# One of the 32 chunks of maxima of a group copied by ACT and folded by Pool

## The reference

```
x = x + attn_a(ln(x))   # 32 heads of 8, biases, plain softmax over 1024 keys
x = x + ffn(ln(x))      # silu gate x up (256 -> 1024), 2:4 sparsified, down
x = x + attn_b(ln(x))   # 32 heads of 8 on 8 key/value heads, -1e10 on keys with i-128 <= j < i
x = x + ffn(ln(x))
```

## Time and profile before

| | us |
|---|---|
| median of 3 runs (1656.22 to 1662.11) | 1660.44 |
| the profiled execution | 1661.54 |
| its span, first to last instruction | 1659.6 |
| PE busy | 1611.3 (97%) |
| DVE busy | 1490.8 (90%) |
| ACT busy | 1282.2 (77%) |
| Pool busy | 267.5 (16%) |

### The profile page before, as it was taken

How to read it: one execution, slowest core, us unless ns; L and a number is a source line. 1 busy time by engine, 2 the same in 40 slices (tenths; PEclk the granted TensorE clock), 3 DMA queues, 4 the chain that set the end, 5 groups by cost and what they waited for, 6 DMA issues and landing times.

```text
span 1659.6 us, 39596 instructions
## 1 busy us (share of the span) xinstructions
PE 1611.3 (97%) x14128; PEld 638.9 (38%) x14128; DVE 1490.8 (90%) x2168; ACT 1282.2 (77%) x2424; POOL 267.5 (16%) x623
## 2 busy tenths in 40 slices
PE   6899999999999999999988999999999999999999
PEld 3322222222222223777753222222222222247777
DVE  6999999999999997787777999999999999938765
ACT  3399999999999998433224999999999999983321
POOL 1410000000000000000012223333322233320000
PEclk9999999999999999999997999999999999999999
DMA  6943344334354321200404322222223222111000
GB/s 161 295 99 70 63 77 83 63 65 84 68 141 87 71 60 44 64 1 1 117 15 132 64 60 57 51 58 60 55 55 67 63 51 52 55 53 55 14 13 26
DMA packets 72126, 114.70 MB, mean 69 GB/s; under 512 B 12464, under 2 KB 27824, under 8 KB 71984
## 3 DMA queue, kind: packets, MB, share of 16 engines
q1 hardware_dynamic: 71984, 112.63, 29.2%
HBM read 71.96 MB, written 40.63 MB: 68 GB/s over the span
## 4 chain that ended last, share of the span: by engine, by line
PE 56%; DVE 32%; issue 7%; DMA 2%; ACT 1%; SPq 1%; DVEq 0%; POOLq 0%; ACTq 0%
DVE mneg L1305 28%; PE psum L785 18%; PE psum L767 11%; PE psum L737 7%; PE psum L887 6%; PE psum L843 6%; PE psum L848 3%; PE psum L700 2%; PE psum L823 2%; DVE area L1355 1%; PE psum L682 1%; PE psum L720 1%; DMA area<-k_stacks 0%; DVE stats L1198 0%; SPq L461 0%
## 5 line engine op out<-in xcount | busy, mean ns | idle before, releaser
L1055 ACT ACTIVATE area<-psum 128x512 f32<-128x512 f32 x2048 | 1097.2, 600 | 42.1 <-PE psum L767 14.6
L785 PE MATMUL psum<-area 128*32 128x256 f32 x8192 | 655.4, 392 | 0.4 <-POOL area L1567 0.4
L767 PE MATMUL psum<-area 51*128 51x512 bf16 x2048 | 638.9, 385 | 2.4 <-DVE vsb_b L1255 1.4
L1311 DVE CUSTOM_DVE_ANT_0 xn<-psum,band 128x1024 f32<-128x1024 f32 x512 | 588.4, 1235 | 12.6 <-PE psum L737 11.3
L1305 DVE TENSOR_REDUCE mneg<-psum 128x1 f32<-128x1024 f32 x512 | 581.0, 1209 | 7.1 <-PE psum L737 7.1
L785 PEld LDWEIGHTS psum<-area 128*32 128x32 f32 x8192 | 162.0, 108 | 400.9 <-issue 259.2
L737 PE MATMUL psum<-area 48*128 48x512 bf16 x1024 | 301.2, 386 | 8.0 <-DVE mneg L1305 4.6
L767 PEld LDWEIGHTS psum<-area 51*128 51x128 bf16 x2048 | 141.1, 94 | 426.5 <-ACT area L1055 353.6
L737 PE MATMUL psum<-k_max_b,area 48*128 48x512 bf16 x1024 | 292.5, 385 | 6.1 <-DVE mneg L1311 5.0
L1548 POOL TENSOR_TENSOR mparts<-mneg,nought 128x16 bf16<-128x16 f32 x64 | 14.2, 222 | 741.6 <-DVE mneg L1305 500.5
L1100 ACT ACTIVATE area<-psum 128x512 f32<-128x512 f32 x64 | 38.2, 600 | 120.0 <-PE psum L848 119.9
(11 more groups left out here) (89 smaller groups left out, 1096.8 us busy)
## 6 DMA issues: line engine op xcount, KB each, us to landing
ctx_rows<-area SPq DMA_DIRECT2D x64, 256.0 KB, 2.1
area<-q_stacks SPq DMA_DIRECT2D x32, 384.0 KB, 6.8
area<-k_stacks SPq DMA_DIRECT2D x64, 192.0 KB, 5.5
area<-q_stacks_b SPq DMA_DIRECT2D x32, 384.0 KB, 5.2
area<-q_stacks SPq DMA_DIRECT2D x32, 192.0 KB, 4.5
area<-q_stacks_b SPq DMA_DIRECT2D x32, 192.0 KB, 3.5
area<-ctx_rows SPq DMA_DIRECT2D x16, 256.0 KB, 3.9
area<-inv_rows SPq DMA_DIRECT2D x16, 256.0 KB, 4.6
```

The source lines that it names most:

```text
L767: pe.matmul(psum[:, BANK_OF["exp", g, u, head], :], k_st[lo:lo + ROWS + PARTS, buf, 0 if a else head // 2, kt * P:(kt + 1) * P], q_st[lo:l ...
L785: mm = pe.matmul(psum[head * VW:(head + 1) * VW, BANK_OF["ctx", g, qh], cols], vaug[:, buf, kt, head, :], probs[:, u % PRING, head, cols], ...
L1055: act.activation(probs[:, u % PRING, head, :], psum[:, BANK_OF["exp", like, u, head], :], ACT.Exp, scale=SCALE).then_inc(bank_freed, 1)
L1311: dve.tensor_tensor_reduce(band_out[:, c % 2, :], slot, band[:, at:at + SEQ], 1.0, -3.0e38, ALU.add, ALU.max, mneg[:, qh, col:col + 1]).th ...
```

## The change

In every group but the first of each attention, chunk 2 (ON_ACT) isn't reduced by DVE. ACT copies its 1024 columns from PSUM to SBUF (`hold`), in unit 4 of the group before, behind the exp of head 1. Pool adds the band (b only) and folds: subtract, maximum with 0, add, which gives the maximum of two halves; three times in a, to 128 columns, and twice in b, to 256. DVE reduces what is left behind chunk 15 (`end_maximum`). PE's wait ahead of chunk 4 is on ACT's copy. The waits on `max_used` are recounted for the new order. `hold_a` lies over the upper weights `wu_hi` (not yet written in attention a), `hold_b` over a part of `xnT`; guards on `narrowed` protect what is written there later.

```diff
+ON_ACT = 2
+ENDED_BEHIND = 15
+STEPS = [c for c in range(ENDED_BEHIND + 1) if c != ON_ACT] + [ON_ACT] + list(range(ENDED_BEHIND + 1, CHUNKS))
+FOLDS = (3, 2)
+def is_held(g, c):
+    return c == ON_ACT and not (isinstance(g, int) and g == 0)
+def maximum_at(a, g, c):
+    return CHUNKS * (GROUPS * a + g) + (c if isinstance(g, int) and g == 0 else STEPS.index(c))
+def held_before(a, g):
+    return (GROUPS - 1) * a + g - 1
...
 # PE, max_scores
-                if not isinstance(g, int) or n >= 2:
-                    pe.wait_ge(max_used, n if in_feed(a, g, c) else n - 1)
+                if in_feed(a, g, c):
+                    pe.wait_ge(max_used, n)
+                elif n >= 2:
+                    G, old = divmod(n - 2, CHUNKS)
+                    layer, h = divmod(G, GROUPS)
+                    if is_held(h, old):
+                        pe.wait_ge(held, held_before(layer, h) + 1)
+                    else:
+                        pe.wait_ge(max_used, maximum_at(layer, h, old) + 1)
...
 # ACT
+            def hold_scores(a, g):
+                k = held_before(a, g)
+                act.wait_ge(max_ready, CHUNKS * (GROUPS * a + g) + ON_ACT + 1)
+                if a and isinstance(g, int):
+                    act.wait_ge(v_done, VBASE[1] + BATCH * VCH[1])
+                if not isinstance(g, int) or k:
+                    act.wait_ge(narrowed, k)
+                bank = max_bank(a, g, ON_ACT)
+                act.copy(hold[a][:], psum[:, bank:bank + 2, :].rearrange("p b c -> p (b c)")).then_inc(held, 1)
...
                                    scale=SCALE).then_inc(bank_freed, 1)
+                    if ahead and head % 2 and LEAD + 2 * u + head // 2 - CHUNKS == ON_ACT:
+                        hold_scores(a, g + 1)
...
 # DVE
-                        dve.wait_ge(max_used, CHUNKS * G + c - 1)
+                        dve.wait_ge(max_used, maximum_at(a, g, c) - (0 if is_held(g, c - 1) else 1))
...
+            def end_maximum(a, g):
+                qh, head, qt = chunk_of(ON_ACT)
+                col = (head % 2) * (CPH // 2) + (head // 2) * (BT // HALF) + qt
+                dve.wait_ge(narrowed, held_before(a, g) + 1)
+                dve.tensor_reduce(mneg[:, qh, col:col + 1], narrow[:, 0:SEQ >> FOLDS[a]], AX.X, ALU.max, negate=(a == 0)
+                                  ).then_inc(max_used, 1)
             def group(a, g):
                 for c in range(CHUNKS):
-                    maxima(a, g + 1, c)
+                    if not is_held(g + 1, c):
+                        maxima(a, g + 1, c)
+                    if c == ENDED_BEHIND:
+                        end_maximum(a, g + 1)
...
 # Pool
+            def band_held(a, g):
...
+                pool.wait_ge(held, held_before(a, g) + 1)
+                pool.tensor_tensor(hold[a][:, cols], hold[a][:, cols], band[:, at + cols.start:at + cols.stop],
+                                   ALU.add).then_inc(held_banded, 1)
+            def fold_held(a, g, i, step):
+                k, n = held_before(a, g), SEQ >> (i + 1)
...
+                near, far = hold[a][:, 0:n], hold[a][:, n:2 * n]
+                last = i == FOLDS[a] - 1
+                if step == 0:
...
+                    pool.tensor_tensor(far, far, near, ALU.subtract).then_inc(held_less, 1)
+                elif step == 1:
...
+                    pool.tensor_scalar(far, far, 0.0, None, ALU.max).then_inc(held_above, 1)
+                else:
...
+                    if last:
+                        pool.tensor_tensor(narrow[:, 0:n], near, far, ALU.add).then_inc(narrowed, 1)
+                    else:
+                        pool.tensor_tensor(near, near, far, ALU.add).then_inc(held_halved, 1)
...
+            HELD_AT = (ON_ACT + CHUNKS - LEAD) // 2
+            FOLD_STEPS = ({HELD_AT: [(i, step) for i in range(FOLDS[0]) for step in range(3)]},
+                          {HELD_AT + 1: [(0, 0)], HELD_AT + 2: [(0, 1)], HELD_AT + 3: [(0, 2)],
+                           HELD_AT + 4: [(1, 0), (1, 1)], HELD_AT + 5: [(1, 2)]})
...
 # Pool, group, at the end of each unit
+                    if ahead and u == HELD_AT and a:
+                        band_held(a, g + 1)
+                    for i, step in FOLD_STEPS[a].get(u, ()) if ahead else ():
+                        fold_held(a, g + 1, i, step)
```

More of the change, by code:

```diff
@@ L194, in hybrid_kernel @@
         wkv_b = [sb(f"wkv_b{i}", [P, DK, KV_HEADS * HD]) for i in range(2)]
+        wu_at = nc.sbuf_base
         wu_hi = sb("wu_hi", [P, DK, INNER // P, P], F32R)
@@ L211, in hybrid_kernel @@
         mT = sb("mT", [CPH * PARTS, HALF, P], BF16)
+        narrow = sb("narrow", [P, SEQ >> 2])
         sums_at = nc.sbuf_base
@@ L276, in hybrid_kernel, with over @@
                  + [parts_mid[:, i] for i in range(2)] + [parts_top[:, 0], parts_far[:, 0]])
-        def over(name, at, shape):
-            return nc.alloc_sbuf_tensor_at(name, shape, F32R, offset=at)
+        def over(name, at, shape, dt=F32R):
+            return nc.alloc_sbuf_tensor_at(name, shape, dt, offset=at)
         wg_hi = over("wg_hi", vsb_at, [P, DK, INNER // P, P])
@@ L289, in hybrid_kernel @@
         xd_lo = [over(f"xd_lo{c}", at, [P, DK, BANK]) for c, (_, at) in enumerate(xd_at)]
+        hold = [over("hold_a", wu_at, [P, SEQ], F32), over("hold_b", xnT_at + 3 * CHUNK_BYTES, [P, SEQ], F32)]
         w_raw = [xnT[:, 2 * i:2 * i + 2].rearrange("p c k t -> p (c k t)").rearrange("p (k n) -> p k n", k=DK)
@@ L332, in hybrid_kernel @@
         mask_started, max_started = sem("mask_started"), sem("max_started")
+        above_started, held_banded = sem("above_started"), sem("held_banded")
+        held, held_less, held_above, held_halved, narrowed = (
+            sem(s) for s in ("held", "held_less", "held_above", "held_halved", "narrowed"))
         x_biased, x_attended, x_fed = sem("x_biased"), sem("x_attended"), sem("x_fed")
@@ L1003, in copy_transposed @@
                     act.wait_ge(whole_split, 2 * DK)
+                if k == 3 and c == 3:
+                    act.wait_ge(narrowed, BATCH * (GROUPS - 1))
                 for tp in range(2):
@@ L1234, in split_dense_weights @@
                 dve.wait_ge(vaug_ready, GROUPS)
+                dve.wait_ge(narrowed, GROUPS - 1)
                 pairs = [(w_raw[i][:, k, :].rearrange("p (h c r) -> p h r c", h=2, r=4),
@@ L1558, in split_max @@
                 pool.tensor_tensor(mparts[:, qh, :, 2, :], view(mres2), view(nought), ALU.add).then_inc(mparts_ready, 1)
+            def band_held(a, g):
+                qh, head, qt = chunk_of(ON_ACT)
+                tile = qh * (BT // HALF) + qt
+                cols = slice(P * max(tile - 1, 0), P * (tile + 1))
+                at = BAND_AT - P * tile
+                pool.wait_ge(held, held_before(a, g) + 1)
[3 more added lines that the diff above has]
+                k, n = held_before(a, g), SEQ >> (i + 1)
+                done = FOLDS[0] * (GROUPS - 1) * a + FOLDS[a] * (g - 1) + i
+                near, far = hold[a][:, 0:n], hold[a][:, n:2 * n]
+                last = i == FOLDS[a] - 1
+                if step == 0:
+                    if i:
+                        pool.wait_ge(held_halved, (FOLDS[0] - 1) * (GROUPS - 1) * a + (FOLDS[a] - 1) * (g - 1) + i)
+                    elif a:
+                        pool.wait_ge(held_banded, g)
+                    else:
+                        pool.wait_ge(held, k + 1)
+                    pool.tensor_tensor(far, far, near, ALU.subtract).then_inc(held_less, 1)
+                elif step == 1:
+                    pool.wait_ge(held_less, done + 1)
+                    pool.sem_inc(above_started, 1)
+                    pool.tensor_scalar(far, far, 0.0, None, ALU.max).then_inc(held_above, 1)
+                else:
+                    if last and (not isinstance(g, int) or g > 1):
+                        pool.wait_ge(max_used, maximum_at(a, g - 1, ON_ACT) + 1)
+                    elif last and a:
+                        pool.wait_ge(max_used, CHUNKS * GROUPS)
+                    pool.wait_ge(held_above, done + 1)
+                    if last:
+                        pool.tensor_tensor(narrow[:, 0:n], near, far, ALU.add).then_inc(narrowed, 1)
+                    else:
+                        pool.tensor_tensor(near, near, far, ALU.add).then_inc(held_halved, 1)
             def mask_probs(a, g, u, ahead):
```

## The result

The changed kernel takes 1689.8 us (median of 4 runs, 1687.7 to 1691.1); before, on the same chip, 1660.9 us. The ratio is 1.0176 (95% interval 1.0162 to 1.0191): slower by 29 us. The prediction said 1691. The profiled execution took 1689.63 us, 28.1 more than that of before, with a span of 1687.9.

A forecast was written before the change was run, and what follows sets the result against it. DVE, back to back, bounds both attentions, with PE's 36.19 us group close behind; +0.99 us (a) and +1.08 us (b) over 15 groups each give 14.9 + 16.2 = +31 us on 1660.44, 1691 us; 8-in-10 range 1662 to 1703.

The forecast's parts named there:

- PE's own group: PE's pace for one group of 32 chunks, without waiting for DVE: 36.19 us, against 36.20 measured in a and 36.63 in b.
- ACT's copy: ACT's 128x1024 copy in unit 4, behind the exp of head 1: 0.91 us, taken from copies of 512 and 128 columns.
- The stall: PE's scores behind unit 5's transposition wait for exps delayed by the copy: PE late by 0.81 us, once per group.
- DVE's idle time cannot be stored: With two slots, DVE idles at chunks 2 to 4 and is behind again from chunk 5: groups 37.2 us (a), 37.7 (b).
- the small reduction: DVE's ending behind chunk 15, over 128 columns in a and 256 in b: 0.21 and 0.34 us added per group.
- The term that was mis-sized: DVE starts a chunk at the earliest 0.82 us after its matmul; used to place chunk 5's reduction at 5.18 us.
- the folds: Pool's folding of the held chunk: under 7 us in a against 13.6 us until DVE asks, so hidden by 6 us.
- Rival 3: Only PE's stall counts, DVE's slots don't: 37.00 us in both attentions, +18 us, 1678; inside the main case's 0.78 chance.
- Rival 1: ACT's idle time and the ring swallow the copy: b falls to 36.19 us, a stays, -6.6 us, 1654; chance 0.11.
- Rival 2: Copy half swallowed, PE's stall about 0.2 us: a +3, b -3, no change, 1660 us; chance 0.07.
- rival 4: Folds late, or Pool and DVE lock each other, costing DVE at least 1.1 us x 30: 1724 us and above; chance 0.04.

## Why the prediction was right, point by point

- **PE's own group.** Forecast 36.19, measured 36.16 where DVE cannot hold it. So nearly nothing (0.04) was to be had in a, and 0.44 (measured 0.47) in b.
- **ACT's copy.** Forecast 0.91 us from the earlier trace rows, measured 0.89, with a record of 1.02. The estimate of 0.95 from the Trainium skill ("ScalarE: Activation LUTs", What ACT_TABLE_LOAD costs) was a little further off.
- **The stall.** Forecast 0.81, measured 0.79. The chain of three banks, exp and 0.19 us of handing over gave 3.00 and 3.48 for the two scores; the trace has 2.97 and 3.46. Moved, halved and quartered copies follow the same rule: 0.52 away from the transposition (0.55 forecast), 0.38 at 512 columns (0.36), nothing at 256 columns in unit 6.
- **DVE's idle time cannot be stored.** Shown from three sides: relief alone gives 0.05 us in b, the copy alone is 7 us better than the whole change, and shorter chunks throughout take b from 37.75 to 36.95. In b the relief even costs, since the small reduction (0.33 us to the next one, forecast 0.34) stands in the part of the group in which DVE is behind, and the chunk taken away in the part in which it waits. The small reduction placed where DVE idles was not tried.
- **The term that was mis-sized.** For a I took 0.82 us from a chunk's matmul to its reduction, a row of attention b. In a it is 245.59 - 244.95 = 0.64. DVE therefore begins its run 0.18 earlier and holds PE back by 0.08 and not by 0.19: a group of 37.03 and not 37.19, +0.83 and not +0.99. In b, where the 0.82 holds (1149.20 to 1150.02), it was 1.12 for a forecast 1.08: chunk 5's reduction starts 0.88 behind its matmul, held by the reduction before it. So a was 2.4 us too high in the sum and b 0.6 too low, 29.3 for 31.
- **Pool.** I had the folds at under 7 us, with a maximum priced like a two-input operation of 1.16. In a they take from 243.09 to 251.91, 8.8 us, as this piece of Pool's timeline shows; DVE asks for the result at 258.05, so 6 us of cover were left and the miss was free. Beside the folds DVE keeps its pace: the eleven reductions from 245.59 on fill 12.54 us, (12.54 - 1.22) / 10 = 1.13 apart. The prediction's remark that by the page's rule each chunk beside the folds would be held goes further than the words that it quotes from the Trainium skill ("Perfetto Trace Analysis", Optimizing Scalar/DVE Operations), which say that such offloading "might not help".

```profile
243.09 1.26 POOL L1644 TENSOR_TENSOR hold_a<-hold_a 128x512 f32<-128x512 f32 x1 [2.22 <-ACT hold_a L1094]
244.55 1.48 POOL L1648 TENSOR_SCALAR hold_a<-hold_a 128x512 f32<-128x512 f32 x1 [0.20 <-POOL hold_a L1644]
...
251.46 0.45 POOL L1656 TENSOR_TENSOR narrow<-hold_a 128x128 f32<-128x128 f32 x1 [0.15 <-DVE mneg L1355]
```

- **The rivals.** Rival 3 (only PE's stall counts) would have been 36.95 in both attentions: 15 x 0.75 + 15 x 0.32 = 16 us, 1677. (The 1672 us of shorter chunks in the changed kernel are less, since they also save time outside these groups.) Rival 1 (the copy is swallowed) is true only of the copy a quarter as long in unit 6. Rival 2 (half swallowed) falls with a stall of 0.79 for its 0.2, rival 4 (Pool late or in DVE's way) with the run without folds.

## What to carry to other kernels

Before moving work off a full engine, work out how long the next engine's own period is, and count the slots between the two: with two slots, an engine relieved once a period idles there and is behind again for the rest of it, while a hundredth of a microsecond off each of its operations was kept in full here. Idle time on the receiving engine is no measure of room either. What counts is how much later one result may come before somebody waits, here 0.24 us against an operation of 0.9, and none at all beside the transposition, where a score already waited.

## What the runs showed of the hardware

Pool's `tensor_scalar` maximum with 0 over 512 columns in place took 1.48 us, longer than the two-input subtraction over as many (1.26), and 0.84 over 256 (the subtraction: 0.73). An ACT copy of 512 columns cost 0.51 us to the next operation out of SBUF and 0.46 out of PSUM. DVE's reductions kept their spacing of 1.13 us beside Pool's folds in a. Their mean record was 1.216 us for 1.209 before; that isn't the folds' doing, since the copy alone, without any folds, has 1.216 too. From a chunk's first matmul to its reduction, where DVE had been waiting, it took 0.64 us in a and 0.82 in b, where the operation also adds the band.
